# Interleaving the row sums with the gathers of a mixture-of-experts block, and moving loads and pads in the block behind it (one core)

## The reference

```python
h = _layernorm(x) * (1 + cb) + sb
logits = einsum('bnc,ec->bne', h, router_w); w, idx = top_k(softmax(logits), 2); w = w / (w.sum() + 1e-9)
out_all[e] = gelu(h @ w1[e].T + b1[e]) @ w2[e].T + b2[e]
x = x + gb * (out_all[idx] * w[..., None]).sum()          # end of layer 0
h = _layernorm(x) * (1 + ca) + sa                          # layer 1
# 16-head attention, and beside it an attention of rank 64 that keeps each row's largest fifth;
# their mix, a small feed-forward, then eight experts with a capacity
```

## Time and profile before

| | us |
|---|---|
| median of three executions | 1414.41 |
| the profiled execution, its time | 1412.28 |
| its span | 1410.6 |
| PE busy | 1275.9 (90%) |
| DVE busy | 1030.0 (73%) |
| ACT busy | 918.1 (65%) |
| POOL busy | 511.8 (36%) |
| L1428 up products, x752, busy | 108.2 |
| L2446 ACT exponentials, x512, busy | 507.2 |
| L158 sends, x64, busy | 64.0 |

### The profile page before, as it was taken

How to read it: one execution, slowest core, us unless ns; L and a number is a source line. 1 busy time by engine, 2 the same in 40 slices (tenths; PEclk the granted TensorE clock), 3 DMA queues, 4 the chain that set the end, 5 groups by cost and what they waited for, 6 DMA issues and landing times. The chain is left out here.

```text
span 1410.6 us, 28627 instructions
## 1 busy us (share of the span) xinstructions
PE 1275.9 (90%) x9145; PEld 817.9 (58%) x9146; DVE 1030.0 (73%) x2720; ACT 918.1 (65%) x1320; POOL 511.8 (36%) x608
## 2 busy tenths in 40 slices
PE   6999768989886778999999999998999989998999
PEld 3877668988863423333334433333434357778898
DVE  5656266667568669888888878888988857787554
ACT  4565523333355487888888878888888848774232
POOL 5337835466449242222201222220122200388800
PEclk9999779999988799999999999999999989999999
DMA  8980112332316722222222222222022014011211
GB/s 258 222 53 24 36 58 87 97 80 72 85 53 232 201 46 37 43 41 39 32 34 33 41 39 41 42 35 38 24 42 37 9 48 139 17 57 57 71 35 32
DMA packets 112673, 93.96 MB, mean 67 GB/s; under 512 B 20034, under 2 KB 98336, under 8 KB 112544
## 3 DMA queue, kind: packets, MB, share of 16 engines
q1 hardware_dynamic: 101192, 76.18, 25.0%
q0 software_dynamic: 6144, 12.73, 3.1%
q10 hardware_dynamic: 5208, 3.43, 1.0%
HBM read 50.40 MB, written 41.89 MB: 65 GB/s over the span
## 5 line engine op out<-in xcount | busy, mean ns | idle before, releaser
L2446 ACT ACTIVATE probs<-scores_ps 128x1024 f32<-128x1024 f32 x512 | 507.2, 1027 | 86.2 <-PE scores_ps L2473 81.5
L2473 PE MATMUL scores_ps<-q_pack,k_pack 64*128 64x512 f32 x1024 | 246.6, 494 | 36.1 <-ACT probs L2446 21.2
L2490 PE MATMUL pv_ps<-probs,v_pad 128*32 128x512 f32 x2048 | 275.9, 611 | 0.0
L2473 PEld LDWEIGHTS scores_ps<-q_pack,k_pack 64*128 64x128 f32 x1024 | 96.2, 185 | 309.6 <-issue 153.5
L2366 POOL TENSOR_TENSOR squares<-sparse_scores 128x512 f32<-128x512 f32 x32 | 41.0, 1280 | 474.2 <-DVE sparse_scores L2611 474.1
L1406 ACT ACTIVATE hidden_experts<-pre_experts 128x512 f32<-128x512 f32 x94 | 59.3, 631 | 130.2 <-DVE pre_experts L1340 66.5
L2683 DVE TENSOR_SCALAR_CACHE_REDUCE junk<-sparse_scores,at 128x1024 f32<-128x1024 f32 x96 | 122.8, 1279 | 3.4
L1428 PE MATMUL up_ps_experts<-x_t_experts,up_weights_now_experts 128*128 128x128 f32 x752 | 108.2, 289 | 16.4 <-issue 7.7
L1428 PEld LDWEIGHTS up_ps_experts<-x_t_experts,up_weights_now_experts 128*128 128x128 f32 x752 | 96.1, 200 | 22.6 <-DVE up_weights_now_experts L1335 11.1
L1435 PE MATMUL down_ps_experts<-weights_t,hidden_experts 128*128 x736 | 100.5, 281 | 0.2 <-issue 0.2
L1435 PEld LDWEIGHTS down_ps_experts<-weights_t,hidden_experts 128*128 128x128 f32 x736 | 92.7, 198 | 0.0
(11 more groups left out here) (416 smaller groups left out, 2493.0 us busy)
## 6 DMA issues: line engine op xcount, KB each, us to landing
q_pack<-q_pieces_dram SPq DMA_DIRECT2D x120, 64.0 KB
k_pack<-k_pieces_dram SPq DMA_DIRECT2D x120, 64.0 KB
expert_rows_dram<-zeros SPq DMA_DIRECT2D x1, 6400.0 KB, 23.0
x_rows_experts<-expert_rows_dram SPq DMA_DIRECT2D x25, 256.0 KB
expert_rows_dram<-y_rows_experts SPq DMA_DIRECT2D x46, 128.0 KB
q_pieces_dram<-q_pieces_prep SPq DMA_DIRECT2D x8, 512.0 KB, 3.6
k_pieces_dram<-k_pieces_prep SPq DMA_DIRECT2D x8, 512.0 KB, 4.1
expert_rows_dram<-zeros SPq DMA_DIRECT2D x1, 2640.0 KB, 40.0
```

Source lines behind the costliest of these rows:

```text
L2446: act.activation(probs[:, kt % 2, 2 * pair : 2 * pair + 2, c * 512 : c * 512 + 512], scores_ps[n % 2][:].rearrange("p (h t) -> p h t", h=2 ...
L2473: ins = pe.matmul(scores_ps[n % 2][:, head * 512 : head * 512 + 512], k_pack[group % 2][rows, pair, kt * P : kt * P + P].bitcast(F32R), q_ ...
L2490: ins = pe.matmul(pv_ps[32 * j : 32 * j + 32, c, :], v_pad[:, group % 2, kt, j, :], probs[:, kt % 2, j, c * 512 : c * 512 + 512], start=(k ...
```

## The change

**Expert block.** `scale_and_shift` of batch 2 becomes eight operations on quarters (256 columns), run by GpSimd at the end of the front (stages `hq`). That of batch 3 becomes eight as well, one behind each of the first eight sends of batch 2. The sums of batches 0 and 1 become ten operations on halves (512 columns). Batch 0's stand one behind each of the gathers 1 to 10 of batch 1; eight of batch 1's follow those gathers, and the last two stand behind gathers 0 and 1 of batch 2, whose tile count begins at 76 (`LAST_FROM`). Both inversions stand behind the last gather. The statistics of batch 0 begin at step 17.

```diff
@@ FRONT_ORDER (last line)
-sd.1.12 sd.1.13 sd.1.14 sd.1.15 wk.10 ce2.3.1 no2.3.1 tu2.3.1 h2t.3.1 lg.3.1 lgk.3.1 be.1 po.1 exps gates ix.1 te.1
+sd.1.12 sd.1.13 sd.1.14 sd.1.15 hq.2.0 hq.2.1 hq.2.2 hq.2.3 hq.2.4 hq.2.5 hq.2.6 hq.2.7 wk.10 ce2.3.1 no2.3.1 tu2.3.1 h2t.3.1 lg.3.1 lgk.3.1 be.1 po.1 exps gates ix.1 te.1
@@ Moe
+    def scale_and_shift_part(self, pool, step, b, i):
+        at = b * NT + i % QUARTERS * (NT // QUARTERS)
+        h = self.h[:, at : at + NT // QUARTERS, :]
+        if i == QUARTERS:
+            step.settle()
+        op, by = ((ALU.mult, CB), (ALU.add, SB))[i // QUARTERS]
+        step(pool.tensor_tensor(h, h, bc(self.mod0[:, b, MOD0_PARTS.index(by), :], NT // QUARTERS), op))
@@ experts0
-    STATS_AT = (13, 20)
+    STATS_AT = (17, 20)
+    ADDED_FIRST, LAST_FROM = 8, 76
...
                     if b >= SENT_EARLY:
-                        moe.scale_and_shift(pool, step, b)
                         step.settle()
-                        moe.send_rows(g, pool, b, apart=next_tile)
+                        for i in range(SEND_PARTS):
+                            moe.send_rows(g, pool, b, i, SEND_PARTS, apart=next_tile)
+                            if b + 1 < B and i < 2 * QUARTERS:
+                                moe.scale_and_shift_part(pool, step, b + 1, i)
...
+                sums = [weighted_sum(g, picked, b, NT // 2) for b in range(EARLY)]
+                def add_up(b):
+                    sums[b].pop(0)(pool, step)
+                    if not sums[b]:
+                        pool.sem_inc(summed, 1)
+                def fetch(b, sem, of, behind):
+                    for i, (n, k) in enumerate([(n, k) for k in range(2) for n in range(NT)]):
+                        gather(pool, g, picked, b, [(k, n)], sem)
+                        next_tile()
+                        if i in behind:
+                            if of == 0 and i == behind[0]:
+                                pool.wait_ge(g.rows_picked, 16 * 2 * NT)
+                            add_up(of)
+                    if behind:
+                        tile_at[0] += 1
+                pool.wait_ge(y_free, 2 * AHEAD + 1)
+                tile_at[0] = max(tile_at[0], moe.tiles)
+                fetch(0, g.rows_picked, None, ())
+                pool.wait_ge(y_free, 2 * (2 * AHEAD) + 1)
+                tile_at[0] = max(tile_at[0], 2 * moe.tiles)
+                fetch(1, g.second_picked, 0, range(1, 11))
+                pool.wait_ge(g.second_picked, 16 * 2 * NT)
+                for _ in range(ADDED_FIRST):
+                    add_up(1)
+                pool.wait_ge(y_free, 3 * (2 * AHEAD) + 1)
+                tile_at[0] = max(tile_at[0], LAST_FROM)
+                fetch(2, g.rows_picked, 1, range(10 - ADDED_FIRST))
+                for b in range(EARLY):
+                    pool.wait_ge(var_ready, b + 1)
+                    g.ln1.invert(pool, b).then_inc(rstd_ready, 1)
+                pool.wait_ge(g.rows_picked, 2 * (16 * 2 * NT))
```

```diff
@@ PREP_ORDER
-kmax.0 qkout.1.1 vk.0 turn.2 bound.0 vout.0 v.1 src.1 root.0 sqk.0 comb.3 ht.2 pads srcout.1 vk.1 q.2 skk.0 vout.1 v.2 p0.2.0 square.2.0 stats.3 k.2
+kmax.0 qkout.1.1 vk.0 turn.2 bound.0 vout.0 v.1 src.1 root.0 sqk.0 combh.3.0 combh.3.1 ht.2 pads srcout.1 vk.1 q.2 skk.0 vout.1 v.2 p0.2.0 square.2.0 stats.3 k.2
-vout.3 first p2.3.1 nq.1 src.3 kmax.1 qkout.3.1 sv.3 bound.1 sqk.3 svk.3 srcout.3 root.1 shift.1 skk.3 p2.3.0 sqd.3 qkout.3.0 srest.1 sqout.3 skc.3
+vout.3 first p2.3.1 nq.1 src.3 kmax.1 qkout.3.1 sv.3 bound.1 sqk.3 svk.3 srcout.3 root.1 shift.1 srest.1 skk.3 late
-vk.2 vout.2 p0.2.1 rest.2.0 square.2.1 shift.0 rest.2.1 rstd.3 p2.2.0 src.2 center.3 qkout.2.0 sqd.0 norm.3 srest.0 sqout.0 sv.2 p2.2.1 turn.3 skc.0
+vk.2 vout.2 p0.2.1 rest.2.0 square.2.1 shift.0 rest.2.1 rstd.3 p2.2.0 src.2 pads1 center.3 qkout.2.0 sqd.0 norm.3 srest.0 sqout.0 sv.2 p2.2.1 turn.3 skc.0
...
-vout.3 first p2.3.1 nq.1 src.3 kmax.1 qkout.3.1 sv.3 bound.1 sqk.3 svk.3 srcout.3 root.1 shift.1 skk.3 p2.3.0 sqd.3 qkout.3.0 srest.1 sqout.3 skc.3
-shout.1
+vout.3 first p2.3.1 nq.1 src.3 kmax.1 qkout.3.1 sv.3 bound.1 sqk.3 svk.3 srcout.3 root.1 shift.1 srest.1 skk.3 late
+warm p2.3.0 shout.1 sqd.3 qkout.3.0 sqout.3 skc.3
@@ combine_and_project
+                    if b == B - 2:
+                        pool.wait_ge(center_ready, nth("center", b + 1))
...
+                def second_pads():
+                    pool.wait_ge(src_ready, nth("src", B - 2))
+                    f.pads(pool, f.k_pack[1], ONE_BITS, pads_ready, 6)
...
+                def combine_half(b, half):
+                    dve.wait_ge((g.half_picked, last_picked)[half], 16 * NT)
+                    sums = weighted_sum(g, picked, b, NT // 2)
+                    for part in sums[half * len(sums) // 2 : (half + 1) * len(sums) // 2]:
+                        part(dve, step)
+                    for part in ln.variance(g, b)[2 * half : 2 * half + 2]:
+                        part(dve, step)
...
+                def warm():
+                    act.activation(warmed[:], g.ident[:, 0:1], ACT.Exp).then_inc(warm_done, 1)
@@ attend
-                            sp.wait_ge(pads_ready, 4)
+                            sp.wait_ge(pads_ready, 2)
...
-                f.pads(pool, 1, pads_ready, 0)
...
                         keep_scores(step, b, group, 0)
+                        if first and group == 0:
+                            wait_stored(dve, *q_whole)
+                            f.pads(dve, q_pack[1], 0, pads_ready, 0)
```

More of the change, by code:

```diff
@@ L615, in scale_and_shift, with scale_and_shift_part @@
                     moe.scale_and_shift(pool, step, b)
+                def scale_and_shift_part(b, i):
+                    if i == 0:
+                        for h in range(2):
+                            wait_made(pool, "tu2", b, h)
+                    moe.scale_and_shift_part(pool, step, b, i)
                 def send(b, q):
@@ L1314, in _ @@
                 pool.sem_inc(rows_here, max(moe.tiles, 2 * UNROLL))
-                for b in range(B - 1):
-                    pool.wait_ge(y_free, b * (2 * AHEAD) + (2 * AHEAD + 1))
-                    tile_at[0] = max(tile_at[0], (b + 1) * moe.tiles)
-                    gather(pool, g, picked, b, [(k, n) for k in range(2) for n in range(NT)], g.rows_picked, apart=next_tile)
-                    if 1 <= b <= EARLY:
-                        pool.wait_ge(var_ready, b)
-                        g.ln1.invert(pool, b - 1).then_inc(rstd_ready, 1)
-                    pool.wait_ge(g.rows_picked, (b + 1) * (16 * 2 * NT))
-                    if b < EARLY:
-                        for part in weighted_sum(g, picked, b, NT):
-                            part(pool, step)
-                        pool.sem_inc(summed, 1)
+                sums = [weighted_sum(g, picked, b, NT // 2) for b in range(EARLY)]
@@ L1551, in __init__ @@
         self.q_pack = [a.sb("q_pack0", [P, 2, T])]
-        self.k_pack = [a.sb("k_pack0", [P, 2, T])]
+        self.k_pack = [a.sb(f"k_pack{i}", [P, 2, T]) for i in range(2)]
         self.v_pad = a.sb("v_pad", [P, 2, NT, 4, 32])
@@ L1583, in load_packs, with pads @@
             ).then_inc(self.packs_loaded[half], 16)
-    def pads(self, pool, half, ready, done):
+    def pads(self, eng, pack, value, ready, done):
         for c in range(2):
             rows = slice(c * HALF_ROWS + SHIFT_ROW, c * HALF_ROWS + HALF_ROWS)
-            for i, (pack, value) in enumerate(((self.q_pack, 0), (self.k_pack, ONE_BITS))):
-                pool.memset(pack[half][rows].bitcast(I32), value).then_inc(ready, 1)
-                pool.wait_ge(ready, done + 2 * c + i + 1)
+            eng.memset(pack[rows].bitcast(I32), value).then_inc(ready, 1)
+            eng.wait_ge(ready, done + c + 1)
     def load_sparse_q(self, sp, scratch, one, group, t):
@@ L1853, in head_masks @@
                     step.settle()
-                walk(PREP_ORDER, dict(pick=pick, rstd=rstds, src=source, pads=pads, heads=head_masks))
+                walk(PREP_ORDER, dict(pick=pick, rstd=rstds, src=source, pads=pads, pads1=second_pads, heads=head_masks))
             @block.vector
@@ L2062, in _ @@
                         first=first_group,
+                        late=first_tiles,
+                        warm=warm,
                     ),
```

31 lines of the change are left out of this document (19 added, 12 removed).

## The result

The changed kernel takes **1408.57 us** (median of 20 runs, 1402.39 to 1413.39) where the kernel before takes 1412.95 (20 runs): a ratio of 0.9973, 95% interval 0.9961 to 0.9984. It is faster by 4 us; 25 were forecast. The profiled execution took 1409.04 us, its span is 1407.1.

What follows compares the result with a forecast made beforehand. TensorE bounds the expert block (busy 193.6 of 210 us), with 28.0 us lost in its loop. Terms 2.5 - 19.0 + 1.2 - 5.4 - 4.3 = -25.0 from median 1414.41 gave 1389.4 us; range 1381 to 1399, with rivals 1380 to 1403.

Steps and rivals of the forecast that it cites:

- End of the front: Before the expert block: batch 2's quarter operations collide with VectorE's last router chain, costing +2.5 us (bounds 0 to 6.0).
- Batch 3's scaling: Expert loop: quarters behind sends keep GpSimd within a tile, the run of five goes; -5.8 us, 0.5 of 6.3 stays.
- Batch 0's sum: Expert loop: -4.6 us of 10.6; 4.5 stays for a run of five gathers, 1.5 for copies waiting beside halves.
- Batch 1's sum and batch 2's gathers: Late expert loop: -8.6 us of 10.6; 1.0 stays for eight halves, 1.0 for the gathers and VectorE's statistics.
- End of the expert block: Behind the last tile: two inversions of up to 1.93 us delay the block's end, +1.2 us (bounds 0 and 2).
- Projecting block: Block after the expert block: `norm.3` 2.2 us earlier, ScalarE's moved loads 3.2 more; -5.4 us (bounds -2 and -8).
- First attention groups: Group 1's start: moved memsets let VectorE's search begin 4 to 6 us earlier; -4.3 us (bounds 0 and -5.4).
- the runs are not the cause: Rival, chance 0.18: expert loop's losses come not from GpSimd's DMA runs; only locked copies are cured, 5.8 of 28.0, giving 1402.6.
- the run that is left does nothing: Rival, chance 0.18: the gather run remaining in the expert loop costs nothing, so 4.5 us more goes, giving 1384.9.
- GpSimd ends the block: Rival, slower, chance 0.01: at the expert block, GpSimd sets the end once a gather with its gap exceeds a tile, 1.93 us.

Runs made afterwards that it cites:

- x7_no_hq: Changed kernel with batch 2's scaling back in the expert block as two 1024-column operations, not in the front: 1397.27 us, ratio 1.0020 to the kernel before, faster chip.
- x1_last72: Changed kernel with LAST_FROM 72 in place of 76, so the last sixteen gathers and both inversions end four tiles earlier: 1399.79 us, ratio 0.9907 to the kernel before.
- x2_run8: Changed kernel with batch 0's gathers 5 to 11 not waiting for `next_tile()`, so nine gathers left in a run: 1416.98 us, ratio 1.0036 to the kernel before.
- x3_spaced: Changed kernel with LAST_FROM 72, an extra tile every third gather-and-half pair, batch 1's ten halves ahead of the last gathers: 1394.32 us, ratio 0.9868.

## Why the prediction was wrong

The traces differ by 3.5 us where 25.0 was forecast. Of the 21.5 missing, 6.8 stand at the end of the expert block, 6.7 in its loop, 6.2 between the next block's begin and the first scores, 1.7 in the rest and 0.1 in the groups.

**End of the front, right.** +2.5 forecast, +2.5 at the first store, +1.9 at the barrier; x7_no_hq agrees, and shows that nothing comes back for it.

**Batch 3's scaling, right with a smaller size.** The run of five is gone; 2.0 of 6.3 stay, not 0.5. Of these 0.75 stand in one step, where three sends follow each other from 215.04 to 218.82 and VectorE waits 1.70 us.

**Batch 0's sum, right in total, by luck in its parts.** 6.0 was to stay, 6.0 stayed, but split otherwise than 4.5 and 1.5 (and the row that 4.5 was taken from gives 6.3 less 1.0, 5.3): 2.4 in the run (four gathers at 321.85 to 326.77, not five), the rest beside the halves, which cost 3.1 in two steps because GpSimd never waits.

**Batch 1's sum and batch 2's gathers, wrong.** The step "the gathers start at tile 76 and go one a tile" left out that two halves stand between the first three gathers. GpSimd comes out of them late, and four gathers leave in a run (changed kernel, order of time):

```profile
362.30 0.96 POOL L1224 DMA_INDIRECT v<-expert_rows_dram,pick  x1 [0.81 <-POOL x L1767]
...
363.57 0.95 POOL L1224 DMA_INDIRECT v<-expert_rows_dram,pick  x1 [0.30 <-issue]
...
364.83 0.95 POOL L1224 DMA_INDIRECT v<-expert_rows_dram,pick  x1 [0.30 <-issue]
...
366.08 0.94 POOL L1224 DMA_INDIRECT v<-expert_rows_dram,pick  x1 [0.30 <-issue]
...
368.22 0.69 DVE L1383 TENSOR_TENSOR pre_experts<-up_ps_experts,weights_t 128x512 f32<-128x512 f32 x1 [1.81 <-remote]
```

The kernel before has the same pattern in the earlier trace rows. With it 6.5 us stay where 2.0 was forecast. These 4.5, the 1.5 at batch 3's scaling and 0.7 at batch 0's undisturbed gathers, which open with a run of three (1.0 lost), are the loop's missing 6.7.

**End of the expert block, wrong, and the largest miss.** "Two inversions of up to 1.93 stand behind it: 3.9 less 2.7" takes GpSimd's last instruction for its end. The block's own line in the trace of before has a drain of 6587 ns at 390.5, hidden by 5.8 us of margin. The margin was 12.4 between that drain's begin and SyncE's (402.9); the change used it up. x1_last72, which only moves the last gathers and the inversions, brings the barrier from 10.4 to 2.7 behind the last store. The term was +8.0, not +1.2. The sum left the drain out; no row shown ahead of it has it.

**Projecting block, wrong.** `root.1` came 2.1 earlier from the block's begin, not 5. Two steps failed. "So `norm.3` and the projections come 2.2 us earlier": `center.3` gained that, and GpSimd, 3.3 later at `rstd.3`, took it back. And the block's end is not what attention waits for: the first scores wait for the packed loads, and begin some 19 us behind the first one's issue (490.0 and 470.9 us). Before, those began 0.3 behind the barrier (87.9 against 87.6), as soon as they could; now 3.0 behind it (88.7 against 85.7), held by loads that left 0.9 later than before. (In the ten profiles with this block the first scores came at 87.1 to 90.0, so +0.8 is no more than "nothing gained".)

**First attention groups, right.** -4.2 for -4.3. These answer to the earlier trace rows; 39.7 us lie between them, where 45.2 did:

```profile
509.45 1.14 ACT L2485 ACTIVATE sparse_exp<-sparse_scores,minus_row_max 128x1024 f32<-128x1024 f32 x1
...
549.15 1.16 ACT L2485 ACTIVATE sparse_exp<-sparse_scores,minus_row_max 128x1024 f32<-128x1024 f32 x1
```

The rival "the runs are not the cause" falls with x2_run8, and "the run that is left does nothing" with it, on the chips where a run of four costs 2.3 or more. The rival that GpSimd ends the block had the right place and the wrong mechanism: its gathers kept to 0.94 to 1.2 us in the loop, and what ended the block was its drain. Nothing slowed TensorE: the granted clock of the stretch is 0.96 (0.95 before).

## What to carry to other kernels

Before work is moved to the end of an engine's share of a block, look at the block's own line: here GpSimd's end was its drain's end, 6.58 us from 394.5 on, and the margin that had hidden it was gone when SyncE ended 9.7 us sooner (393.2 for 402.9). A paced queue must be able to catch up: when GpSimd is late, its tokens are all there and its gathers leave in a run, and four of them cost 4.2 us here behind tile 76; with a skipped pace it waits again, and batch 0's ten half operations cost 1.0 where they cost 6.0 (x3_spaced). And an edit that moves a barrier is worth only what the wait behind the barrier leaves: this one came 1.9 us nearer the block's begin (85.7 for 87.6), and the first scores 0.8 later (88.7 for 87.9).

## What the runs showed of the hardware

- GpSimd's closing drain of the expert block took 6.58 to 6.68 us in every profile, whether an inversion or a gather stood last. In the changed kernel its drain took 2.68 in the front, behind the quarters, and 0.06 at the end of attention (1109.2), 0.1 us behind its last instruction; in the expert block SyncE's took 0.013, VectorE's 0.35, ScalarE's 0.52 and TensorE's 1.97.
- In the expert loop the other engines stand still beside gathers 0.30 us apart (x2_run8: TensorE 6.96 us, ScalarE 5.86, VectorE 2.99): on the slower chips a step of the loop lost 0.5 to 2.6 us with three in a run, 2.3 to 4.3 with four, 9.2 with nine; on the faster chip at most 0.4 with three, 0.8 to 1.2 with four, and 0.6 with four and a fifth 0.35 us behind. The same gathers in pairs, with a wait of 1.5 us between pairs (after, 273 to 294 us), cost at most 0.2 in a step. It is not so everywhere: in the front of the kernel before, nine sends left 0.30 us apart (165.23 to 176.40) and no engine shows a nameless wait beside them.
- Beside ten half operations in step with the tiles a 128x512 copy took a median of 418 ns (x3_spaced, 293 to 322 us); beside drifting ones 1120 ns (changed kernel).
- The memset of 32x2048 on VectorE took 1.76 us (494.93 in the changed kernel), and so about what it took on GpSimd (1.80).
- The same kernel took 1393 us on one chip and 1411 to 1414 on three others.
